# Windowed attention: context with queries as rows, values and scores in one block, and new orders on all five engines

## The reference

```python
for l in range(6):
    q, k, v = split(x @ Wqkv[l])                  # 16 heads of width 64
    q = rotary(l2norm(q) * q_scale); k = rotary(l2norm(k) * k_scale)
    # windows of 32 queries; each sees its own 32 keys and the 32 before
    sim = where(mask, -max, einsum(q, k) * 8)
    x = einsum(softmax(sim), v) @ Wo[l] + x
    a, g = split(layernorm(x) @ W1[l] + b1[l])    # inner width 341
    x = (a * gelu(g)) @ W2[l] + b2[l] + x
```

## Time and profile before

| | before |
|---|---|
| median of 3 runs | 3864.42 us (3851.44 to 3864.74) |
| the profiled execution | 3854.79 us, its span 3853.0 us |
| PE busy | 3672.5 us (95%) |
| DVE busy | 3196.5 us (83%) |
| POOL busy | 3063.6 us (80%) |
| ACT busy | 2919.4 us (76%) |
| mean granted clock of PE | 0.984 |

### The profile page before, as it was taken

How to read it: one execution, slowest core, us unless ns; L and a number is a source line. 1 busy time by engine, 2 the same in 40 slices (tenths; PEclk the granted TensorE clock), 3 DMA queues, 4 the chain that set the end, 5 groups by cost and what they waited for, 6 DMA issues and landing times. The chain is left out here.

```text
span 3853.0 us, 176449 instructions
## 1 busy us (share of the span) xinstructions
PE 3672.5 (95%) x66944; PEld 2523.9 (66%) x66944; DVE 3196.5 (83%) x6391; ACT 2919.4 (76%) x6003; POOL 3063.6 (80%) x3927
## 2 busy tenths in 40 slices
PE   4999997899999999999999999999999999999997
PEld 2344443567777777777777777777777777777775
DVE  6888884788888888888888888888888888888885
ACT  6466666677777887778777777787778777778874
POOL 5111112989999999999999999999999999999993
PEclk7899999999999999999999999999999999999998
DMA  3433221222222322223222232222232222222222
GB/s 95 61 37 39 39 26 48 79 66 63 64 62 73 83 65 65 65 65 94 65 65 64 63 91 63 64 65 65 71 89 65 65 62 64 73 63 65 65 66 57
DMA packets 179255, 250.64 MB, mean 65 GB/s; under 512 B 46902, under 2 KB 69940, under 8 KB 178228
## 3 DMA queue, kind: packets, MB, share of 16 engines
q1 hardware_dynamic: 179124, 248.92, 26.7%
HBM read 39.07 MB, written 8.39 MB: 12 GB/s over the span
## 5 line engine op out<-in xcount | busy, mean ns | idle before, releaser
L1135 PE MATMUL w_ring<-shared,w_xs 128*128 (+1 forms) x2304 | 1157.3, 605 | 10.0 <-ACT w_xs L1325 4.7
L1540 POOL TENSOR_TENSOR w_qr<-w_raw,w_tc 128x512 f32<-128x512 f32 x384 | 489.0, 1273 | 146.4 <-PE w_ring L1155 138.3
L1554 POOL TENSOR_TENSOR w_qr<-w_qr,w_qrot 128x512 f32<-128x512 f32 x384 | 575.6, 1499 | 0.0
L1135 PEld LDWEIGHTS w_ring<-shared,w_xs 128*128 128x128 f32 x2304 | 378.8, 191 | 176.9 <-issue 143.6
L1547 POOL TENSOR_TENSOR w_qrot<-w_raw,w_tc 128x512 f32<-128x512 f32 x384 | 486.3, 1277 | 0.0
L1217 PEld LDWEIGHTS w_ring<-w_pts,w_vw 64*64 64x64 f32 x24576 | 377.0, 135 | 94.2 <-issue 94.1
L693 ACT ACTIVATE a_probs<-a_wide 128x512 f32<-128x512 f32 (+1 forms) x608 | 314.4, 581 | 156.5 <-PE a_wide L601 154.0
L733 POOL TENSOR_SCALAR_AFFINE_SELECT a_probs<-a_probs 128x512 f32<-128x512 f32 x128 | 81.6, 638 | 441.6 <-ACT a_probs L693 441.6
L764 DVE TENSOR_REDUCE a_row_max<-a_ring 128x1 f32<-128x512 f32 (+3 forms) x608 | 360.9, 654 | 85.2 <-PE a_ring L580 60.4
L1332 ACT ACTIVATE w_ksq<-w_ring 128x512 f32<-128x512 f32 x384 | 229.4, 598 | 251.6 <-PE w_ring L1135 251.6
L1217 PE MATMUL w_ring<-w_pts,w_vw 64*64 64x32 f32 x24576 | 398.6, 220 | 5.2 <-issue 3.5
(11 more groups left out here) (171 smaller groups left out, 8631.0 us busy)
## 6 DMA issues: line engine op xcount, KB each, us to landing
w_vw<-w_v SPq DMA_DIRECT2D x1152, 128.0 KB, 2.3
w_vw<-w_v SPq DMA_DIRECT2D x768, 64.0 KB, 2.0
shared<-in_L_ffn_Wqkv SPq DMA_DIRECT2D x6, 1536.0 KB, 6.0
shared<-q_parts SPq DMA_DIRECT2D x108, 64.0 KB
shared<-k_parts SPq DMA_DIRECT2D x108, 64.0 KB
q_parts<-ap_parts SPq DMA_DIRECT2D x8, 384.0 KB, 4.4
k_parts<-ap_parts SPq DMA_DIRECT2D x8, 384.0 KB, 5.0
shared<-in_L_ffn_Wo SPq DMA_DIRECT2D x12, 256.0 KB, 3.2
```

The costliest lines, as they stand in the source:

```text
L1135: nc.tensor.matmul(bank(what, i, u)[:], xs[u][:], rhs, start=True, stop=True).then_inc(done, 1)
L1540: nc.gpsimd.tensor_tensor(by_head(qr[i][:]), by_head(raw[i][:]), wide(table(u, Q_COS)), ALU.mult).then_inc(q_straight[i], 1)
L1554: nc.gpsimd.tensor_tensor(qr[i][:], qr[i][:], qrot[i][:], ALU.add).then_inc(q_added[i], 1)
```

## The change

- **Context.** The value products are turned round: the probabilities are the weights (64 keys x 32 queries) and v the moving side (64 columns), so the context has queries as rows. It is then divided by the row sums (`normalise_o`, DVE, from PSUM into the new tile `o`) and transposed by four products (`turn_o`, PE) before `store_c`. `divide` is gone; `turn_p` waits for the exp alone.
- **Block.** `scores` and `values` are one call, `block(r, u)`: the values of the chunk before, then mask and scores, behind one set of waits.
- **Moves.** `carry` goes from POOL to ACT. The first step of `refine` (`ssc`) goes to ACT as an Identity in `factor_log`. `copy_v` no longer reorders its columns.
- **Orders.** `body` is rewritten on PE, ACT, POOL and DVE, with a new `USES`, and `LAG` is 4 in place of 6. `ffn_out(pair - 5)` near the start is now `ffn_out(pair - 4)` at the end. On ACT, the gelus no longer stand together.

```diff
-                chunk(pe, divided[e], r, u)
+                chunk(pe, exped[e], r, u)
...
-                hold(pe, landed, 2 * r + (u + 1), *[bank_before("ct", par, u, r)[1] for par in range(2)])
+            def block(r, u):
+
+                rv, uv = (r, 0) if u == 1 else (r - 1, 1)
...
-                                                      vw[u][keys, w, at:at + HD], pts[e][keys, n, BAND * w:BAND * (w + 1)],
-                                                      start=True, stop=True)
+                def value(n, e):
+                    for w in range(4):
+                        for par in range(2):
+                            rows, keys, at = slice(BAND * w, BAND * (w + 1)), slice(HD * par, HD * (par + 1)), P * n + HD * e
+                            mm = nc.tensor.matmul(bank("ct", par, uv)[rows, at:at + HD], pts[e][keys, n, rows], vw[uv][keys, w, at:at + HD],
+                                                  start=True, stop=True)
+                    return mm
...
+                if has_values:
+                    for n in range(4):
+                        for e in range(2):
+                            vm = value(n, e)
+                    vm.then_inc(valued, 1)
+                if has_scores:
+                    mask()
+                    for j in range(8):
+                        sm = score(j)
+                    sm.then_inc(scored, 1)
+
+            def turn_o(r, u, par):
...
+                for n in range(4):
+                    mm = nc.tensor.transpose(out[:, n * P:(n + 1) * P], o[par][:, n * P:(n + 1) * P], t.ident[:])
+                mm.then_inc(o_flipped[par], 1)
...
+                nc.scalar.activation(ssc[:], over[:], ACT.Identity, bias=tiny[:, 0:1]).then_inc(floored, 1)
...
+            def carry(r, u):
...
+                factor = keep[:, bass.ds(r % PAIRS_B, 1)] if u == 0 else 1.0
+                nc.scalar.activation(kt[u][:, :, 0:BAND], kt[1 - u][:, :, P:KEYS], ACT.Copy, scale=factor).then_inc(carried, 1)
...
-                nc.vector.tensor_tensor(p[u][e][:], p[u][e][:], per_head(rinv[:, 8 * e:8 * e + 8]), ALU.mult).then_inc(divided[e], 1)
+                nc.vector.tensor_tensor(o[par][:].rearrange(split, n=4, e=2), bank("ct", par, u)[:].rearrange(split, n=4, e=2), factor, ALU.mult
+                                        ).then_inc(o_ready[par], 1)
```

More of the change, by code:

```diff
@@ L1156, in turn_q @@
                 mm.then_inc(q_flipped[i], 1)
[L1158 to L1183, removed]
-                            mm = nc.tensor.matmul(bank("sc", e, u)[rows, WIN * j:WIN * (j + 1)], qt[u][d, j, rows],
-                                                  kt[u][d, j, BAND * w:BAND * w + WIN], start=False, stop=True, skip_group_check=True)
-                mm.then_inc(scored, 1)
             def turn_p(r, u, e):
@@ L1464, in body @@
             def body(pair):
-                copy_v(pair - 2, 1, 0)
+                exps(pair - 2, 0, 1)
+                exps(pair - 2, 0, 0)
                 copy_v(pair - 2, 1, 1)
-                store_c(pair - 3, 1, 1)
+                carry(pair - 2, 1)
+                store_kt(pair - 2, 1, 1)
                 square_k(pair - 1, 0, 0)
-                store_kt(pair - 2, 1, 1)
-                store_qt(pair - 2, 1, 1)
+                store_kt(pair - 2, 1, 0)
                 build_xs(pair - 1, 1)
@@ L1473, in body @@
                 factor_log(pair - 1, 0)
+                store_p(pair - 2, 0, 1)
+                store_qt(pair - 2, 1, 1)
+                store_qt(pair - 2, 1, 0)
                 build_xf(pair - 3)
+                store_p(pair - 2, 0, 0)
                 factor_seed(pair - 1, 0)
[L1476 to L1477 removed]
+                square_q(pair - 1, 1, 0)
+                carry(pair - 1, 0)
+                var_log(pair - 3)
                 copy_v(pair - 1, 0, 0)
[L1479 removed]
@@ L1492, in body @@
-                choose_rows(pair - 1)
-                build_xs(pair, 0)
-                square_k(pair - 1, 1, 0)
                 store_c(pair - 2, 0, 0)
                 store_c(pair - 2, 0, 1)
+                square_k(pair - 1, 1, 0)
+                copy_v(pair - 1, 0, 1)
+                exps(pair - 2, 1, 0)
+                store_qt(pair - 1, 0, 1)
+                gelu(pair - 3, 1)
+                clamp(pair - 1, 1)
+                exps(pair - 2, 1, 1)
+                factor_log(pair - 1, 1)
@@ L1497, in body @@
+                gelu(pair - 3, 0)
+                choose_rows(pair - 1)
                 store_kt(pair - 1, 0, 1)
-                gelu(pair - 3, 0)
-                gelu(pair - 3, 1)
-                store_kt(pair - 1, 0, 0)
-                store_qt(pair - 1, 0, 1)
+                build_xs(pair, 0)
+                gelu(pair - 3, 2)
                 store_qt(pair - 1, 0, 0)
-                gelu(pair - 3, 2)
-                square_q(pair, 0, 0)
-                clamp(pair - 1, 1)
-                factor_log(pair - 1, 1)
@@ L1507, in body @@
-                factor_seed(pair - 1, 1)
-                copy_q(pair, 0, 0)
                 store_p(pair - 2, 1, 1)
                 store_p(pair - 2, 1, 0)
-                exps(pair - 1, 0, 0)
-                square_k(pair, 0, 1)
-                exps(pair - 1, 0, 1)
+                store_kt(pair - 1, 0, 0)
+                factor_seed(pair - 1, 1)
+                square_q(pair, 0, 0)
                 square_q(pair, 0, 1)
                 copy_q(pair, 0, 1)
+                square_k(pair, 0, 1)
@@ L1516, in body @@
                 store_c(pair - 2, 1, 0)
+                copy_q(pair, 0, 0)
+                copy_v(pair - 1, 1, 0)
+                store_c(pair - 2, 1, 1)
             nc.scalar.preload_act_table_set("natural_log_exp_and_others")
```

240 lines of the change are left out of this document (128 added, 112 removed), and 12 rows, old and new, of the table USES.

## The result

The kernel before took 3861.21 us (median of 4 runs here, 3851.44 to 3864.74), the changed one 4497.52 us (4 runs, 4497.25 to 4499.25). The ratio is 1.1654, with a 95% interval of 1.163 to 1.1677: slower by 636 us. I had forecast 4470, range 4290 to 4640.

A forecast was written before the change was run, and what follows sets the result against it. A cycle through PE, ACT's loads ahead of xs, and PE again was taken as the bound: 4.8 plus 1.7 for the half clock, 6.5 a pair over 94 pairs, 611 us on 3854.8, gives 4470, range 4290 to 4640.

The forecast's parts named there:

- The place and the chain: PE's first projection waits for xs behind four of ACT's five loads: stand 4 us, period 37.3, +4.8 a pair.
- rival 1: Same chain through ACT's loads and xs, but the half clock costs nothing: 4306 us; chance 0.22.
- The base: Loop period of the kernel before, counted from 77 table loads in 2500 us: 32.47 us a pair.
- The block: Values, mask and scores on PE: 1.40 + 0.39 + 1.40 = 3.19 us, with value products at the scores' rate.
- rival 2: Longer chain: value products stay at 2.00 (4580 us), or the slow stretch is 6.8 us long (4630); chance 0.18.
- The clock: Half rate on PE behind each 4 us stand costs 1.7 us a pair, bounds 0 and 3.4.
- The loads: ACT has five table loads an iteration, 1.30 us each, where before had two; three more are 3.9.
- rival 5: On ACT a table load also drags a drain, at most as long as a load: 4830 or 4860 us; chance 0.03.
- Rival 3: ACT's loads cost nothing on the path, PE bounds: 3855 us, 20 either way; needs xs 4.0 earlier; chance 0.04.
- PE alone: PE's own work goes to 32.3 to 32.4 us a pair (-0.1), with 1.76 added for four turns of o.
- Rival 4: Loads cost nothing and PE's remaining waits go too, to 31.9 us a pair: 3800 us; chance 0.03.
- LAG: LAG 4 in place of 6 unrolls fewer bodies, outside the steady loop: nothing.

The follow-up runs named there:

- e4: Changed kernel with four added 512-column products on PE, in its stand ahead of the wait for xs: 4312.81 us, ratio 1.1191.
- e6: Kernel before with only three added table loads on ACT, ahead of choose_rows and build_xs: 4039.21 us, ratio 1.0478.
- e3: Changed kernel with the set for both exp and Ln loaded behind gelu 1 too, so Ln needs no own load: 4324.52 us, ratio 1.1207.
- e1: Changed kernel with ACT's gelus together behind build_xs, two table loads an iteration, and DVE's gate 1 later: 3967.19 us, ratio 1.0293.
- e2: Changed kernel with only build_xs of the next pair moved ahead of gelu 1 on ACT, five loads left: 4458.87 us, ratio 1.1566.
- e9: e1 with gelu 1 ahead of build_xs and choose_rows behind gelu 0 on ACT, banks unchanged: 3934.95 us, ratio 1.0203.
- e10: e9 with turn_o transposing one of its four blocks (output not the reference's): 3919.03 us, ratio 1.0166.
- e5: e1 with gelu 1, choose_rows and copy_q moved on ACT, turn_k ahead of feed-forward part 0 on PE, two banks swapped: 4050.86 us, ratio 1.0507.
- e7: e5 with LAG 6, as in the kernel before, in place of 4: 4073.39 us, ratio 1.057.

## Why the prediction was right, and where its terms were off

**The place and the chain: right.** The chain in terms of the prediction, with what the trace after shows: PE from block to end of the k projection, then ACT starts `square_k`, 19.8, measured 2039.13 - 2019.47 = 19.66. ACT from there to the end of `xs` 2.9 + 10.75 = 13.65, measured 2052.56 - 2039.13 = 13.43. From the end of `xs` PE's start comes 0.45 later (2053.01), a step that the sum didn't have; the two stretches ahead of it, 0.14 and 0.22 too long in the sum, nearly make up for it. Stand of PE 4, measured 4.05. From there to the block 3.8, measured 3.81 in e4. Period without clock loss 37.3, measured 37.22 in e4, where the clock stays at 1.00 in the loop: 4312.8, beside the 4306 that rival 1 gave for just this case. DVE, POOL and the windows of v were no bound, as said; the 0.7 that I gave to a wait for gate 1 came as 0.72 for another step of DVE (`w_kr`), ahead of the stand.

**The base: too short.** The prediction took 32.47 a pair for before, and the period is 32.58. So the chain's loss is 4.64 a pair and not 4.8.

**The block: too long in my sum.** I gave values, mask and scores 1.40 + 0.39 + 1.40 = 3.19. They take 2022.38 - 2019.47 = 2.91. The value products do run at the scores' rate (1.43 and 1.48 to the next start, weights 105 ns both), so the first half of rival 2 is out. The mask products, which in the earlier trace rows took 0.39 by themselves, hardly show here. Two blocks make 0.56 too much, and gaps between other steps, beyond the 0.4 that the sum had for changes of tile size, gave most of it back (0.18 behind the second turn of o and 0.38 ahead of the second block are the largest), so 19.8 came out nearly right by errors of opposite sign. That part was luck.

**The clock: mis-sized, inside its bounds.** I had 1.7, from one stretch of 3.4 us at half rate. e4 puts it at 2.0. The reason shows in the rows: in every second iteration the slow stretch is 6.80 us, of which some 1.3 lie in the stand, and in the others 3.4. The work from `xs` to the block takes 2026.44 - 2022.63 = 3.81 in e4, at full rate. In the changed kernel it takes 2019.47 - 2013.15 = 6.32 and 2058.18 - 2053.01 = 5.17: losses of 2.5 and 1.4, on average 1.9. A doubled stretch was my second half of rival 2; it comes in half of the iterations. Rival 1, a slow stretch that falls into the stand, is out. Why the two lengths alternate no run shows. The rule that I cited from the Trainium skill, TensorE: Matmul & The Clock Gate, section "HAM oscillation — how this bites in real kernels" (half rate after each stand of a loop, and half of the throttled time lost), agrees with these stands of 4 us: on the path the slow stretches are some 5.5 and 3.1 us long, and half of that is 2.1 on average.

**The loads: right in price and place.** Each costs 1.29 to 1.30 us and nothing more: three in a row are 3.86 in e6, nothing stands between the copy, the load and the gelu (2044.13, 2045.42), and the one taken out in e3 shortened the stand by 1.42, where rival 5's load would have taken 2.6. The Trainium skill, ScalarE: Activation LUTs, section "What ACT_TABLE_LOAD costs", puts a drain of some 1380 ns on top of a load; these rows don't show it. The same page of the Trainium skill, section "Table sets: the hidden batching unit", advises to batch by table set. e1 did that and put `xs` ahead of the loads, and both together gave 530 of the 636 us. Most of it is the batching: e2, with `xs` ahead of all five loads, gave 39, and e9, with one of its two loads ahead of `xs` again, is 32 us faster than e1. Rival 3 said that `xs` 4 us earlier would free the loop. e2 shows that this isn't enough: what stands beside `xs` behind the loads has to come earlier too.

**PE alone: not shown.** I had 32.3 to 32.4. e9 is at 33.21, and comes to 32.43 only if the two "issue" waits of the blocks, 0.54, could go; if they are PE's own, it is 32.97, 0.6 above the forecast. And e10 says that the 1.76 for four turns of o can't be taken as their price on the path, since two of them lie where ACT's copy of q would hold PE anyway. As an estimate from e9's waits, a kernel without them would come to 3935 - 0.78 x 94 = 3862, or to 3912 without the one for xb alone; the first equals the kernel before and doesn't beat it. Neither was built. Rival 4 (3800) has nothing for it.

**LAG: put at nothing, and worth about 20 us on e5.** I counted it at nothing, and e7 against e5 shows 22 us outside the steady loop. In the changed kernel the periods give (39.25 - 32.58) x 94 = 627 of the 636 us, so 9 are left for all that lies outside, the shorter LAG among it. LAG by itself wasn't measured there, and the cause of the 22 us stays open.

The sum of 4466 was low by some 31 us. The clock was 31 too low, what lies outside the loop 9, and the kernel before was 6 above the 3854.8 that I built on; the chain was 15 too high. That the miss is so small is in part luck, as these errors partly cancel; the chain and its place are not.

## What to carry to other kernels

Count a table load where it stands, by who waits for what is queued behind it, and not by its engine's idle share: ACT was busy for three quarters of the time and still cost PE 4.6 us a pair. When a wait is found, list everything else behind the same cause before moving the one thing that is named; the next in line is as late, and a ring of buffers has more such waits than it names. A stand of PE costs more than its length when half clock follows on the path, and cheap work in the stand shows how much.

## What the runs showed of the hardware

- With a stand of 4.05 us of PE in each iteration the granted clock was at 0.50 for 3.4 and 6.8 us by turns. Four added products in the stand kept it at 1.00 (e4). Stands of 1.4 to 1.5 us in every iteration (e5, e6) left the loop at 0.99 and 1.00, stands of 2.6 and 2.7 (e3, e2) gave 0.96 and 0.94.
- The value products with 64x32 weights and 64 moving columns take 1.43 us where 64x64 and 32 took 2.00, for the same products, with 105 ns a load of weights in place of 135.
- An exp that follows a gelu and an Ln that follows the exp had a load each (2046.12 and 2048.07), though one set serves both: in e3, where that set was asked for ahead of the exp, four loads an iteration were left.
